# Cross-attention kernel: the sums of y's blocks made by accumulating DMAs from HBM instead of GpSimd additions

## The reference

```python
x_q = einsum('oc,bcn->bno', w_qk, y)
x_k = einsum('oc,bcn->bon', w_qk, x)
x_v = einsum('oc,bcn->bon', w_v, x) + b_v
energy = einsum('bnc,bcm->bnm', x_q, x_k)
attention = softmax(energy, -1)
attention = attention / (1e-07 + attention.sum(axis=1, keepdims=True))
x_r = einsum('bcn,bnm->bcm', x_v, attention)
return x + relu(einsum('oc,bcn->bon', w_t, x - x_r) + b_t)
```

## Time and profile before

| what | value |
|---|---|
| time, two executions | 1847.73 and 1849.26 us, median 1848.49 us |
| span of the profiled execution | 1846.8 us |
| PE busy in it | 1841.7 us |
| PEld busy | 1553.5 us |
| DVE busy | 1499.5 us |
| ACT busy | 1310.9 us |
| POOL busy | 788.0 us |
| moved by DMA | 101.92 MB, mean 55 GB/s |

### The profile page before, as it was taken

One profiled execution on the slowest core, in us unless ns is written; L12 is line 12 of the kernel. 1 busy time (PEld: TensorE's weight loads), 2 busy tenths in 40 slices (PEclk: granted clock), 3 DMA queues, 4 the chain that ended last, 5 costly groups with the idle time before them and its releaser, 6 DMA issues.

```text
span 1846.8 us, 26440 instructions
## 1 busy us (share of the span) xinstructions
PE 1841.7 (100%) x8901; PEld 1553.5 (84%) x8901; DVE 1499.5 (81%) x2034; ACT 1310.9 (71%) x1799; POOL 788.0 (43%) x422
## 2 busy tenths in 40 slices
PE   9999999999999999999999999999999999999999
PEld 8888888888888888888888888888888888888887
DVE  7878787787887877878878788787787877878777
ACT  7767776677666786667776677766677666776665
POOL 5543344432444424444244452444533444334431
PEclk9999999999999999999999999999999999999999
DMA  3201111011110111101111111111011110111101
GB/s 108 68 25 57 58 68 68 23 68 46 68 68 23 68 46 68 68 33 58 46 68 68 48 43 46 68 68 61 30 48 66 68 68 23 64 50 68 68 1 46
DMA packets 34090, 101.92 MB, mean 55 GB/s; under 512 B 4224, under 2 KB 5248, under 8 KB 34048
## 3 DMA queue, kind: packets, MB, share of 16 engines
q1 hardware_dynamic: 33760, 101.07, 15.8%
q10 hardware_dynamic: 288, 0.39, 0.1%
HBM read 67.90 MB, written 33.55 MB: 55 GB/s over the span
## 4 chain that ended last, share of the span: by engine, by line
PE 98%; DVE 1%; ACT 0%; issue 0%; POOL 0%; DVEq 0%; ACTq 0%; POOLq 0%
PE pv L796 37%; PE row_b L691 19%; PE row_a L691 14%; PE pv L768 9%; PE row_b L754 5%; PE row_a L754 5%; PE row_a L745 5%; PE row_b L745 5%; DVE colsum L536 0%; PE pv L898 0%; PE pv L754 0%; PE pv L931 0%; PE pv L902 0%; ACT p_sb L336 0%; DVE z_lo L503 0%
## 5 line engine op out<-in xcount | busy, mean ns | idle before, releaser
L218 POOL TENSOR_TENSOR y_lo<-y_raw,y_hi 128x896 fp32r<-128x896 f32 (+1 forms) x128 | 277.1, 2190 | 546.7 <-ACT y_hi L297 357.1
L543 DVE SCALAR_TENSOR_TENSOR p_lo<-p_sb,row_inv,p_hi 128x1024 fp32r<-128x1024 f32 x254 | 325.4, 1282 | 96.0 <-ACT p_hi L344 95.9
L327 ACT ACTIVATE ev<-row_b 128x512 f32<-128x512 f32 x384 | 229.5, 598 | 199.7 <-PE row_b L691 199.1
L203 POOL TENSOR_TENSOR x_lo<-x_sb,x_hi 128x1024 fp32r<-128x1024 f32 x63 | 152.2, 2415 | 449.2 <-ACT x_hi L280 449.2
L336 ACT ACTIVATE p_sb<-p_sb,neg_max 128x1024 f32<-128x1024 f32 x256 | 295.1, 1154 | 28.6 <-DVE neg_max L518 24.6
L344 ACT ACTIVATE p_hi<-p_sb,row_inv 128x1024 fp32r<-128x1024 f32 x256 | 292.4, 1143 | 30.7 <-PE pv L796 30.0
L536 DVE SCALAR_TENSOR_TENSOR colsum<-p_sb,row_inv,colsum 128x1024 f32<-128x1024 f32 x224 | 291.7, 1302 | 8.5 <-DVE row_inv L526 0.6
L796 PE MATMUL pv<-p_hi,z_hi 128*128 128x512 f32 x1024 | 273.7, 389 | 0.0
L796 PE MATMUL pv<-p_hi,z_lo 128*128 128x512 f32 x1024 | 273.7, 389 | 0.0
L518 DVE CUSTOM_DVE_ANT_0 p_sb<-row_a,ev 128x1024 f32<-128x1024 f32 x128 | 156.6, 1223 | 143.6 <-PE row_a L691 143.6
L796 PE MATMUL pv<-p_lo,z_hi 128*128 128x512 f32 (+1 forms) x1047 | 271.7, 383 | 0.0
(11 more groups left out here) (157 smaller groups left out, 3585.9 us busy)
## 6 DMA issues: line engine op xcount, KB each, us to landing
x_sb<-x SPq DMA_DIRECT2D x64, 512.0 KB, 4.6
out<-res SPq DMA_DIRECT2D x62, 512.0 KB, 3.4
y_raw<-y SPq DMA_DIRECT2D x64, 256.0 KB, 3.7
y_raw<-y SPq DMA_DIRECT2D x32, 512.0 KB, 3.7
out<-res SPq DMA_DIRECT2D x2, 256.0 KB, 2.1
res<-w_qk SPq DMA_DIRECT2D x1, 256.0 KB, 3.0
res<-w_t_T SPq DMA_DIRECT2D x1, 256.0 KB, 6.7
res<-w_v SPq DMA_DIRECT2D x1, 256.0 KB, 7.8
```

What stands on the lines that cost most here:

```text
L218: nc.gpsimd.tensor_tensor(y_lo[:, of:, cols], y_raw[:, 1 + of:8, cols], y_hi[:, of:, cols].bitcast(FP32), ALU.subtract).then_inc(y_lo_done, 1)
L327: nc.scalar.activation(ev[:, to, :], bank_b, ACT.Copy, scale=scale).then_inc(b_copied, 1)
L543: nc.vector.scalar_tensor_tensor(out=p_lo[r][:, :], in0=p_sb[r][:, :], scalar=row_inv[:, j:j + 1], in1=p_hi[r][:, :].bitcast(FP32), op0=AL ...
```

## The change

For batches 1 to 31 POOL no longer adds. SP's first load now copies the upper right block into four slots (4 to 7) at once, reading it four times from HBM (a source with a repeated dimension): 1024 KB in place of 256 KB. Slot 0 is used only in the first batch. Then POOL issues three DMAs with `accum_op=ALU.add`, each of which reads HBM and adds to what stands in SBUF: the lower right block to slots 4, 5, 6 (768 KB), the upper left block to slots 5, 6, 7 (768 KB), and the lower left block to slot 6 (256 KB). They touch the same slots, so each waits for the one before (semaphore `y_added`). `y_high` waits for the third. Slots 6 and 7 change places (`Y_S3`, `Y_S4`).

```diff
-Y_A11, Y_A12, Y_A22, Y_S1, Y_S2, Y_S3, Y_S4 = range(7)
+Y_A11, Y_A12, Y_A22, Y_S1, Y_S2, Y_S4, Y_S3 = range(7)
...
+    def repeated(ap, n):
+        return ap.rearrange("p (a n) -> p a n", a=1).to_broadcast([P, n, BANK])
...
-            def load_y(b):
-                sp.dma_start(y_raw[:, 0, :], y_dram[b][:, 0, BANK:N]).then_inc(y_in, DMA)
+            def load_y(b, first=False):
+                if first:
+                    sp.dma_start(y_raw[:, 0, :], y_dram[b][:, 0, BANK:N]).then_inc(y_in, DMA)
+                else:
+                    sp.dma_start(y_raw[:, 4:8, :], repeated(y_dram[b][:, 0, BANK:N], 4)).then_inc(y_in, DMA)
...
             def y_sums(b):
                 pool.wait_ge(y_in, 3 * DMA * (b + 1))
-                nc.gpsimd.tensor_tensor(y_raw[:, 4, :], y_raw[:, 0, :], y_raw[:, 3, :], ALU.add).then_inc(summed, 1)
-                nc.gpsimd.tensor_tensor(y_raw[:, 6, :], y_raw[:, 0, :], y_raw[:, 1, :], ALU.add).then_inc(summed, 1)
-                pool.wait_ge(summed, 4 * b + 1)
-                nc.gpsimd.tensor_tensor(y_raw[:, 5, :], y_raw[:, 4, :], y_raw[:, 1, :], ALU.add).then_inc(summed, 1)
-                pool.wait_ge(summed, 4 * b + 3)
-                nc.gpsimd.tensor_tensor(y_raw[:, 7, :], y_raw[:, 5, :], y_raw[:, 2, :], ALU.add).then_inc(summed, 1)
+                pool.dma_start(y_raw[:, 4:7, :], repeated(y_dram[b][:, 1, BANK:N], 3),
+                               accum_op=ALU.add).then_inc(y_added, DMA)
+                pool.wait_ge(y_added, DMA * (3 * b - 2))
+                pool.dma_start(y_raw[:, 5:8, :], repeated(y_dram[b][:, 0, 0:BANK], 3),
+                               accum_op=ALU.add).then_inc(y_added, DMA)
+                pool.wait_ge(y_added, DMA * (3 * b - 1))
+                pool.dma_start(y_raw[:, 6, :], y_dram[b][:, 1, 0:BANK],
+                               accum_op=ALU.add).then_inc(y_added, DMA)
...
             def y_high(b, t, first=False, sums=False):
                 of, cols = 3 if sums else 0, slice(t * P, (t + 1) * P)
-                act.wait_ge(summed, 4 * (b + 1))
-                if not first:
+                if first:
+                    act.wait_ge(summed, 1)
+                else:
+                    act.wait_ge(y_added, 3 * DMA * b)
                     act.wait_ge(row_b_done, NP * (b - 1) + t + 1)
```

More of the change, by code:

```diff
@@ L137, in xattn_kernel @@
         x_lo_done, y_lo_done = sem("x_lo_done"), sem("y_lo_done")
+        y_added = sem("y_added")
         summed, t3_made, t_lo_done = sem("summed"), sem("t3_made"), sem("t_lo_done")
@@ L183, in _ @@
                 load_x(0, 0, kt)
-            load_y(0)
+            load_y(0, first=True)
             sp.dma_start(wtT_sb, by_channel(w_t_T)).then_inc(weights_in, DMA)
@@ L250, in _ @@
                                     ALU.subtract).then_inc(a_lo_done, 1)
-            nc.gpsimd.tensor_tensor(y_raw[:, 7, :], y_raw[:, 5, :], y_raw[:, 2, :], ALU.add).then_inc(summed, 4)
+            nc.gpsimd.tensor_tensor(y_raw[:, 6, :], y_raw[:, 5, :], y_raw[:, 2, :], ALU.add).then_inc(summed, 1)
             t_three(0)
@@ L657, in _ @@
             nc.vector.tensor_tensor(y_raw[:, 4, :], y_raw[:, 0, :], y_raw[:, 3, :], ALU.add).then_inc(setup_y, 1)
-            nc.vector.tensor_tensor(y_raw[:, 6, :], y_raw[:, 0, :], y_raw[:, 1, :], ALU.add).then_inc(setup_y, 1)
+            nc.vector.tensor_tensor(y_raw[:, 7, :], y_raw[:, 0, :], y_raw[:, 1, :], ALU.add).then_inc(setup_y, 1)
             dve.wait_ge(setup_y, 1)
```

## The result

The changed kernel takes 2141.39 us (median of 2139.95 and 2142.83) against 1848.49 us before: a ratio of 1.159 (95% interval 1.157 to 1.161), 293 us slower. The prediction was 2008 us, range 1847 to 2170. Direction, place and range held; the loss is nearly twice the 159 us forecast, and the time lies above the forecast's own band of 1920 to 2090 us.

The account below looks back on a forecast made before the run. PE, busy for 1841.7 of 1846.8 us, was taken as the bound. Late sums cost 30 x 4.95 = 148.5 us, plus 11 in the first batch: 159.5 us more, a 2006.3 us span, 2008 us measured, range 1847 to 2170.

Parts of the forecast that it names:

- lateness of the sums: At ACT's y_high of tile 0: the sums are ready 6.1 us after their use at 833.07, each batch.
- less 1.15 us: Slack in ACT's queue behind y_high, before PE's p6 of pair 2: ACT can be 1.15 us late at no cost.
- The forecast's own account: Sums late at ACT's y_high by 3 to 9 us, giving 1920 to 2090 us; chance 0.49.
- the clock: Rival: PE's pauses let its clock fall to 1.2 GHz, costing 75 to 150 us on top of 2008; chance 0.10.
- The larger load: SP's y loads move 786 KB more in 2.3 us; y is there 1.4 us later than POOL started before.
- First accumulating DMA: On POOL's queue, 768 KB: about 7.4 us from issue to landing, with doubled data time and 1.0 us for issue.
- Neighbours: SP's stores and x loads share the DMA engines with the second accumulating DMA, which loses 1.5 us (0 to 3.4).
- Third: The last accumulating DMA on POOL's queue, 256 KB: about 4.4 us from issue to landing.
- The first batch: Load and use of y are tighter there: sums 12.6 us late, counted as 11 us lost.
- The two pauses: PE in pair 2, each batch: p1 late by 3.0 us through DVE's maximum, p6 adding 1.9 us through ACT's copy.
- Hidden: Rival: accumulating DMAs run like plain loads, 10.8 us, ahead of ACT's use; only the first batch loses; 1851 us, chance 0.25.
- Dear issues and crowded engines: Rival: POOL takes 2.4 us per DMA issue and the second DMA loses 3.4 us; 2199 us, chance 0.15.

Follow-up runs that it names:

- e2: The changed kernel with SP's two stores and two x loads held back until the third accumulating DMA has landed; 2028.91 us, ratio 1.098.
- e3: The changed kernel with its three POOL DMAs as plain copies of the same bytes, additions left out; 1924.84 us, ratio 1.042.
- e5: The changed kernel with 24 unused matmuls more in each of 30 batches, in PE's pause ahead of p1 of pair 2; 2123.93 us, ratio 1.148.
- e6: As e3, but the three plain copies are issued by SP's queue instead of POOL's; 1855.02 us, ratio 1.004.
- e7: Changed kernel with y_high of tile 0 in pair 2 (first batch: both after pair 3), POOL's y_low of tile 0 after both x_low; 1871.30 us, ratio 1.013.
- e8: As e7, but POOL's y_low of tile 0 runs between the two x_low instead of after them; 1855.32 us, ratio 1.004.

## Why the prediction was right, and what it mis-sized

**The place and the law of the loss** held. The forecast was: lateness of the sums, less 1.15 us, once a batch. ACT's wait ahead of `y_high` gives the lateness. The lost time is the average period less 57.20 us, read over 29 periods as above.

| kernel | ACT's wait a batch | less 1.15 us | lost a period |
|---|---|---|---|
| changed | (308.8 - 12.0) / 30 = 9.9 us | 8.7 us | 66.66 - 57.20 = 9.5 us |
| e2 | 183.8 / 30 = 6.1 us | 5.0 us | 62.73 - 57.20 = 5.5 us |
| e3 | (107.0 - 6.5) / 30 = 3.4 us | 2.2 us | 59.41 - 57.20 = 2.2 us |
| e5 | (315.8 - 12.4) / 30 = 10.1 us | 9.0 us | 66.20 - 57.20 = 9.0 us |
| e6 | none | none | 57.18 - 57.20 = 0 us |

e3 and e5, whose mean clocks are 1.00 and 0.99, fit to a tenth. The 0.5 to 0.8 us more in the first two go with a mean clock of 0.94 and 0.96.

**The range held by room kept for rivals.** The forecast's own account, sums late by 3 to 9 us, ends at 2090 us; the sums were 9.9 us late and the time was 2141. That number lies in the span that the prediction gave to "the clock", whose mechanism was worth 17 us. The three DMAs together took 23.1 us in the period shown, inside the 17.8 to 23.4 us of the forecast; the later y, the first batch and the clock took the time beyond its band.

**The terms of the sum:**

- The larger load, +1.4 us: it came 8.8 us after SP's first issue instead of 7.1. The data took what was forecast: DMA shares of 5.57 us for 1835 KB, 329 GB/s. The end was too early. I had let the last load land 3.8 us after its issue, plus 2.3, 6.1 in all; the median landing in the changed kernel's period is 6.9 us, and GpSimd begins 0.8 us after that. I had put that last step at nothing, though the earlier trace rows have POOL starting at 817.12, 0.9 us after the 816.2 that I took for the landing. 1.7 us missed.
- First accumulating DMA, forecast 7.4: 7.8 us, of which 4.6 data and 1.0 GpSimd (e6 against e3) are as forecast, and the remaining 2.2 were taken as 1.8.
- **The term most mis-sized** is "Neighbours": "at half the rate the second would lose up to 3.4 us, at no loss 0; I take 1.5 us". It lost 3.9 us in the period shown and 3.5 us on average (e2), which is the upper end and not its middle. Since y and the first DMA were 2.1 us late, it was issued at 963.23 - 135.22 = 828.0 on the clock of the earlier trace rows, where I had 825.9, and its data met SP's from the start (the stretch 965 to 966 moved 283 GB/s, above the 170 of an accumulating DMA alone) instead of from the middle. SP's transfers were slowed too: x loads took 8.1 us instead of 4.6 (medians).
- Third, forecast 4.4: 4.0 us.
- 1.7 + 0.4 + 2.4 - 0.4 = 4.1 us more, which is 10.2 instead of 6.1. That is where most of the loss beyond the forecast comes from: about 4 us in each of 30 batches.
- The first batch, forecast 11 us: 12.5.

**The two pauses.** I expected `p1` and then `p6` to wait. There was one pause, 7.27 us ahead of `p1` (10.2 - 3.1 = 7.1 by the forecast's own numbers). The second was filled by the slow matmuls at half the clock; e5, at the full clock, has both. "The clock" as a rival of its own was priced at 75 to 150 us and was worth about 17 for that reason; the fall itself came.

**The rivals.** "Hidden" is out by e3 against the changed kernel, though e6 shows that plain copies from SP would have made it. "Dear issues and crowded engines" was half right: the engines were crowded and the issues weren't dear (1.3, 1.3 and 0.9 us). The rule of the Trainium skill for a DMA from GpSimd ("DMA: Bandwidth & Descriptors", the anatomy of one DMA) gives 3.8 us for 786 KB as an estimate, which is below what was measured: 5.4 us for a plain copy from GpSimd and 7.8 us with accumulation. The Trainium skill, "Collectives: The Full Stack", section on the bandwidth ceiling, states half the rate where a reduction reads two sources over one ring, and says it of collectives; the 4.61 us of data time here, against 2.15 us for the plain copy of e3, agree.

## What to carry to other kernels

Work moved off an engine that has time to spare gained nothing here, and the chain that replaces it has to meet the same deadline: write down when the value is used and what stands behind the user in its queue, and subtract the slack of the next wait; the rest is lost each time. A chain of transfers that wait for one another is priced per transfer (here 4.4, 5.4 or 7.8 us for 786 KB), and where it crosses other traffic it takes longer (here 3.5 us on average beside 2.1 MB). When such a chain is late by a fixed amount, move the use before you try to make the transfers faster: here one instruction of ACT was worth 272 us.

## What was not expected

- GpSimd and DVE can hold each other up: a DVE pass with two SBUF inputs that started 0.3 us into a GpSimd pass took 2.87 instead of 1.28 us, and the place of one GpSimd instruction was worth 16 us of the kernel (e7 against e8). The Trainium skill, "SBUF — State Buffer", section "Who interferes with whom", states this as an exclusive lock between a DVE instruction with two SBUF inputs and a GpSimd instruction that reads SBUF; these rows agree.
- A period whose deadline is set by DMAs varies, from 64.4 to 69.4 us, where the kernel before keeps to 57.1 to 57.3 us. Crowding isn't the whole reason, since e2's periods still vary from 61.5 to 64.8 us; the rest stays open.
- PE at half the clock was nearly free, since it filled time in which PE would have waited for ACT.
